# Single-tile experts: the down product in plain fp32, its weights read in place at a register's address

## The chip, the cores and the metric

One Trainium2 chip, one of its NeuronCores. The metric is the device time of one execution in microseconds. Engines are called TensorE (PE, with its weight loads as PEld), VectorE (DVE), ScalarE (ACT), GpSimd (POOL) and SyncE (SP, which issues DMAs).

## The reference

The kernel computes four stages on x (16 blocks of 128 rows, 256 wide) with a context of the same shape, each added to x after a layer norm: a masked context product, a transformer block whose feed-forward part has 8 experts (top 2), a cross-attention, and a second layer of 16 experts (top 2) with a shared one. The change lies in the first layer of experts:

```
w = vals / jnp.sum(vals, axis=-1, keepdims=True)          # vals, idx: top 2 of 8
gate = jnp.sum(jax.nn.one_hot(idx, E) * w[..., None], axis=1)
hid = silu(einsum('td,edf->tef', t, w1)) * einsum('td,edf->tef', t, w3)
y_e = einsum('tef,efd->ted', hid, w2)                     # the down product
y = einsum('ted,te->td', y_e, gate)
```

t has 2048 rows of 256, an expert is 512 wide. All is fp32.

## The kernel before

Rows are sorted by expert through DRAM, and each tile of 128 rows is computed for one expert only. The first layer (r = 0) has NT0 = 39 tiles. The first PAIRED = 18 go in pairs that share weights; the 21 after them (j = 18 to 38) are the single tiles. Which expert a tile has is known only at run time: TI[j, 0] holds its number, and an engine that needs it loads it into a register (value_load) and addresses the weights with it. WGU and WD hold the gate/up and the down weights of all experts in SBUF.

A single tile goes through these phases:
- SP: xs fetches the tile's rows.
- PE: xT transposes them (2 matmuls, lines 954 and 955); ACT: xT_e copies the result (L1332).
- ACT and DVE: wa and wv (L1307, L1855) copy the two halves of the expert's gate/up weights, scaled by g2, into one of two buffers; both wait for up(j-2) and then load the expert's number.
- PE: gate and up, eight plain fp32 matmuls each (L982).
- ACT: silu (L1338); DVE: hm multiplies it with up into H_ (two buffers, L1879).
- The split: ACT rounds the weights of down (wdh, L1316) and the hidden values (hh, L1350) to fp32r, and DVE takes the remainders (wdl, L1872, and hl, L1888). There is one buffer for the split weights.
- PE: down adds three fp32r products for each of four k (mm3, L788 to L790) in one bank.
- DVE: y copies the bank out (L1896); SP: ys stores it to DRAM.

The order of the work on each engine is fixed when the program is built. A planner (Plan.order, lines 144 to 196) keeps a clock for each engine and takes, over all engines, the phase with the least sum of its earliest start and its due time. A phase's due time is 3j plus its entry in LEAD: 100 for xT, gate and up, 300 for hm, 200 for wv, 300 for wa, -17200 for xT_e; down has none. A phase's successor on another engine is ready when it has ended and 200 more (170 after DVE) have passed, on the same engine after 60. The costs are nanoseconds written in the code; they set nothing but the order:

```
k = min(starts, key=lambda k: starts[k] + phases[k][4])
t = starts[k]
engine, ns, _, banks, _, late = phases[k]
```

PSUM has eight banks; in this stage xT, gate, up and down have two each, and a bank is used again when its reader has emptied it.

After the last single tile comes the cross-attention. Its K and V products (lines 1031 and 1041, by mm3) can begin beside the last tiles, in two banks that K_e and V_e (L1416, L1426) empty into buffers which lie on top of WD; the first of these evictions wait for wdl(38), the last reader of WD. Q needs x, so it waits for the experts' results: all y stored, then gathered by GpSimd (ga, L2148), weighted and normed (pro1, pro2: L1938, L1941, L1957), transposed (NT).

Of the kernel before, what the change touches and what calls it, by code (L numbers as in the profile page):

```python
# [12 lines left out]
ACT = mybir.ActivationFunctionType  # L13
# [3 lines left out]
D = 256  # L17
# [106 lines left out]
class Plan:  # L124
# [9 lines left out]
    def add(self, engine, ns, key, *after, banks=(), due=0, late=None):  # L134
        after = [k for k in after if all(not isinstance(i, int) or i >= 0 for i in k)]
        name = (engine, key[0], key[1] if key[0] in BY_STAGE else 0)
        due += LEAD.get(key[0] + str(key[1]) if key[0] in BY_STAGE else key[0], 0) + NUDGE.get(key, 0)
        if name in self.latest:
            after.append(self.latest[name])
        self.latest[name] = key  # L140
        assert key not in self.phases, key
        self.phases[key] = (engine, ns, after, banks, due, LATE.get(engine, 200) if late is None else late)
# [141 lines left out]
def expert_phases(p, r, start):  # L284
    F, n = F_[r], 2 * F_[r]
    nd, ny = ((1, 3), (2, 3))[r]
    for j in range(NT_[r]):
        def add(engine, ns, name, *after, banks=(), **kw):
            p.add(engine, ns, (name, r, j), *after, banks=[(ring + str(r), (q, r, j)) for ring, q in banks],
                  due=3 * j, **kw)  # L290
        begin = start if j == 0 else []
        add("SP", 1000, "xs", ("xT", r, j - 3), *([("ix", r, j - 3)] if r else []), *begin, late=28000 if r and j < 3 else 2200)
        if not r and j < PAIRED:
            j0 = j - j % 2
            add("ACT", 960, "wa", ("up", r, j - 2), *begin)
            add("DVE", 1145, "wv", ("wa", r, j))
            if j == j0:
                add("ACT", 960, "wdh", ("down", r, j - 1), *begin)
                add("DVE", 1145, "wdl", ("wdh", r, j))
            add("PE", 220, "xT", ("xs", r, j), banks=[("xT", "xTl")])  # L300
            add("ACT", 310, "xTh", ("xT", r, j), ("up", r, j0 - 3))
            add("DVE", 420, "xTl", ("xTh", r, j))
            p.add("PE", 1440, ("gate", r, j), ("xTl", r, j0), ("wv", r, j), ("xTl", r, j0 + 1), banks=[("gate0", ("silu", r, j))], due=3 * j)
            add("PE", 1440, "up", ("gate", r, j), banks=[("up", "hm")])
            add("ACT", 470, "silu", ("gate", r, j), ("hl", r, j - 2))
            add("DVE", 600, "hm", ("up", r, j), ("silu", r, j))
            add("ACT", 520, "hh", ("hm", r, j), ("down", r, j0 - 1))
            add("DVE", 600, "hl", ("hh", r, j))
            add("PE", 1440, "down", ("hl", r, j0 + 1), ("wdl", r, j0), banks=[("down", "y")])
            add("DVE", 345, "y", ("down", r, j), *([("ys", r, j - ny)] if j >= ny else []))  # L310
            add("SP", 60, "ys", ("y", r, j), late=2000)
            continue
        add("ACT", 100 + 0.84 * n, "wa", ("up", r, j - 2), *begin)
        add("DVE", 60 + 0.6 * n, "wv", ("up", r, j - 2), *begin)
        add("ACT", 100 + 0.84 * n, "wdh", ("down", r, j - nd), *begin)
        add("DVE", 70 + 1.04 * n, "wdl", ("wdh", r, j))
        add("PE", 220, "xT", ("xs", r, j), banks=[("xT", "xT_e")])
        add("ACT", 270, "xT_e", ("xT", r, j), ("up", r, j - 2))
        add("PE", 3.52 * F, "gate", ("xT_e", r, j), ("wv", r, j), ("wa", r, j), banks=[("gate", "silu")])
        add("PE", 3.52 * F, "up", ("gate", r, j), banks=[("up", "hm")])  # L320
        add("ACT", 62 + 0.79 * F, "silu", ("gate", r, j), ("hl", r, j - 2))
        add("DVE", 70 + 1.04 * F, "hm", ("up", r, j), ("silu", r, j))
        add("ACT", 90 + 0.84 * F, "hh", ("hm", r, j), ("down", r, j - 1))
        add("DVE", 70 + 1.04 * F, "hl", ("hh", r, j))
        add("PE", 2.82 * F, "down", ("hl", r, j), ("wdl", r, j), banks=[("down", "y")])
        add("DVE", 330, "y", ("down", r, j), *([("ys", r, j - ny)] if j >= ny else []))
        if r:
            add("DVE", 100, "ix", ("xs", r, j), *([("te",)] if j == 0 else []))
            add("POOL", 1100, "ys", ("y", r, j), ("ix", r, j), late=2000)
        else:  # L330
            add("SP", 60, "ys", ("y", r, j), late=2000)
# [7 lines left out]
def cross_phases(p):  # L339
    p.add("SP", 100, ("load_kv",), ("down", 0, PAIRED - 1), due=0, late=12000)  # L340
    p.add("SP", 100, ("load_q",), ("down", 0, NT0 - 1), late=8000)
    p.add("ACT", 100, ("tanh",), ("load_kv",), ("hh", 0, NT0 - 1))
    p.add("DVE", 330, ("btg",), ("tanh",))
    over = [("wa", 0, NT0 - 1), ("wv", 0, NT0 - 1)]
    for j in range(-1, NB // 2):
        due = 3 * (j + 1)

        def add(engine, ns, key, *after, banks=(), **kw):
            p.add(engine, ns, key, *after, banks=banks, due=due, **kw)
# [16 lines left out]
        for u in range(2):  # L366
            n = 2 * j + u
            if j in EARLY_KV:
                add("SP", 60, ("kl", n), ("S", 2 * (n - 3) + 1), late=2500)
                for h in (4 * j + 2 * u, 4 * j + 2 * u + 1):  # L370
                    add("SP", 60, ("vl", h), ("PV", h - 7), late=2500)
                continue
            for half in range(2):
                add("PE", 1440, ("K", j, u, half), ("kwl", u), ("cl", j), ("S", 2 * (n - 3) + 1), banks=[("proj", ("K_e", j, u, half))])
                add("ACT", 466, ("K_e", j, u, half), ("K", j, u, half), ("S", 2 * (n - 3) + 1), *([("wdl", 0, NT0 - 1)] if n < 3 else []))
            for i in range(2):
                add("PE", 1380, ("V", j, u, i), ("vwl", u), ("K", j, 0, 0), ("PV", 4 * j + 2 * u + i - 7), banks=[("proj", ("V_e", j, u, i))])
                add("ACT", 466, ("V_e", j, u, i), ("V", j, u, i), ("PV", 4 * j + 2 * u + i - 7), *([("wdl", 0, NT0 - 1)] if 4 * j + 2 * u + i < 7 else []))
        for b in (2 * j, 2 * j + 1):
            add("POOL", 2550, ("ga", 0, b), ("ys", 0, NT0 - 1), ("places",), ("pro1", b - 2),  # L380
                late=4000 if b < 2 else 2800)
# [109 lines left out]
def program(nc, a, out):  # L491
    with ExitStack() as ctx:
# [135 lines left out]
        def done(*key):  # L628
            return S[SIGNAL[key[0]]], ORD[key]
# [162 lines left out]
        def tensor(pe):  # L792
# [193 lines left out]
            def down(r, j):  # L986
                F, n, D_ = F_[r], 2 * F_[r], WDN_[r]
                vacant(pe, "down", r, j)
                hT, wd, at, step = HT_[r][0], D_[j % len(D_)], 0, 128
                if paired(r, j):  # L990
                    pe.wait_ge(*done("hl", r, j - j % 2 + 1))
                    pe.wait_ge(*done("wdl", r, j - j % 2))
                    hT, at, step = HTP, 128 * (j % 2), 256
                else:
                    pe.wait_ge(*done("hl", r, j))
                    pe.wait_ge(*done("wdl", r, j))
                for k in range(F // 128):
                    i = mm3(pe, ps("down", r, j)[:, 0:D],
                            [hT[:, (i * F // 128 + k) * step + at:(i * F // 128 + k) * step + at + 128] for i in range(2)],
                            [wd[:, i * n + k * D:i * n + k * D + D] for i in range(2)], k == 0, k == F // 128 - 1)  # L1000
                i.then_inc(*fills("down", r, j))
# [195 lines left out]
        def scalar(act):  # L1197
# [136 lines left out]
            def silu(r, j):  # L1334
                act.wait_ge(*full("gate", r, j))
                if j >= 2:
                    act.wait_ge(*done("hl", r, j - 2))
                act.activation(H_[r][j % 2], ps("gate", r, j)[:, 0:F_[r]], ACT.Silu).then_inc(*frees("gate", r, j))  # L1338

            def hh(r, j):  # L1340
# [68 lines left out]
            def K_e(jj, u, half):  # L1409
                n = 2 * jj + u  # L1410
                act.wait_ge(*full("K", jj, u, half))
                if n >= 3:
                    act.wait_ge(*full("S", 2 * (n - 3) + 1, i=1))
                else:
                    act.wait_ge(*done("wdl", 0, NT0 - 1))
                act.copy(kT_[n % 3][:, half * 512:half * 512 + 512],  # L1416
                         ps("K", jj, u, half)[:, :]).then_inc(*frees("K", jj, u, half))

            def V_e(jj, u, b2):
                n = 4 * jj + 2 * u + b2  # L1420
                act.wait_ge(*full("V", jj, u, b2))
                if n >= 7:
                    act.wait_ge(*full("PV", n - 7))
                else:
                    act.wait_ge(*done("wdl", 0, NT0 - 1))
                act.copy(xv_[n % 7], ps("V", jj, u, b2)[:, :]).then_inc(*frees("V", jj, u, b2))  # L1426

            def Q_e(jj, u, half):
# [954 lines left out]
```

## Time and profile before

| what | value |
|---|---|
| median of 3 runs | 919.88 us (916.21 to 920.40) |
| span of the profiled execution | 928.5 us; the page gives no other time of it |
| TensorE busy | 863.3 us, 93% of the span |
| VectorE, ScalarE, GpSimd busy | 710.4, 607.8, 278.9 us |
| single tiles of the first experts | 299 to about 411 us of the span |

Times in the rows are microseconds from the start of the span. Busy is the sum of an engine's instructions; a matmul's record lasts longer than its spacing, because matmuls are pipelined, so the distance between starts is what one costs. One plain fp32 matmul of the program leaves two records. "Idle before <- releaser" is the time that the engine stood still ahead of an instruction and what ended it; "issue" is a wait for which the profile shows no releaser.

### The profile page before, as it was taken

How to read it: one execution, taken by the hardware profiler on the slowest of the kernel's cores; microseconds unless marked ns; L12 is line 12 of the kernel's file. 1: busy time of each engine (PE TensorE's matmuls, PEld its weight loads, DVE VectorE, ACT ScalarE, POOL GpSimd, SP SyncE). 2: the span in 40 equal slices, each digit the busy share in tenths (PEclk: the TensorE clock that was granted, in tenths of full speed). 3: DMA queues.
4: the chain of work that ended last, by engine and by line, in shares of the span. 5: the costliest groups of instructions: out<-in, count | busy, mean ns of one | idle time of the engine just before them, and what ended most of it. 6: DMA issues, size and time to landing. Idle time of an engine off the chain costs nothing.

```text
span 928.5 us, 23435 instructions
## 1 busy us (share of the span) xinstructions
PE 863.3 (93%) x7788; PEld 771.5 (83%) x7788; DVE 710.4 (77%) x1976; ACT 607.8 (65%) x1719; POOL 278.9 (30%) x359
## 2 busy tenths in 40 slices
PE   5899988758999999998899999999999999999997
PEld 3677666437999999997799988899888989999996
DVE  5888888656898666675788888977678548888867
ACT  4488899735766666665667676677766326777740
POOL 4755578640000000004432333511113102333320
PEclk9999999958999999999999999999999999999999
DMA  9145701611111411103100122121024952333335
GB/s 327 64 177 217 291 25 36 264 55 52 52 62 55 149 53 46 53 24 127 39 24 24 45 84 58 62 66 35 25 102 161 412 123 87 99 96 102 99 117 196
DMA packets 43031, 97.11 MB, mean 105 GB/s; under 512 B 6080, under 2 KB 28480, under 8 KB 41504
## 3 DMA queue, kind: packets, MB, share of 16 engines
q1 hardware_dynamic: 36048, 76.81, 23.8%
q0 software_dynamic: 6864, 18.80, 5.8%
q8 instruction: 64, 1.05, 0.5%
q14 instruction: 55, 0.45, 0.2%
HBM read 62.22 MB, written 33.37 MB: 103 GB/s over the span
## 4 chain that ended last, share of the span: by engine, by line
PE 64%; DVE 7%; issue 3%; ACT 2%; another core or an unknown queue 1%; POOL 1%; DMA 1%; ACTq 0%; DVEq 0%; POOLq 0%
PE ps L982 17%; PE ps L788 11%; PE ps L790 10%; PE ps L789 10%; PE ps L1099 3%; PE ps L1075 3%; PE ps L1085 3%; PE ps L1157 2%; DVE BIGR L1903 1%; PE ps L954 1%; PE ps L955 1%; ACT BIG L1443 1%; DVE BIG L1980 1%; DVE X L1938 1%
## 5 line engine op out<-in xcount | busy, mean ns | idle before, releaser
L788 PE MATMUL ps<-BIGR 128*128 128x256 f32 (+1 forms) x970 | 299.0, 308 | 10.5 <-DVE BIGR L1903 3.9
L790 PE MATMUL ps<-BIGR 128*128 128x256 f32 (+1 forms) x922 | 263.4, 286 | 0.0
L789 PE MATMUL ps<-BIGR 128*128 128x256 f32 (+1 forms) x746 | 219.2, 294 | 0.0
L788 PEld LDWEIGHTS ps<-BIGR 128*128 128x128 f32 x970 | 186.0, 192 | 20.1 <-issue 16.1
L982 PE MATMUL ps<-BIG 128*128 128x128 f32 x1424 | 180.5, 275 | 0.0
L790 PEld LDWEIGHTS ps<-BIGR 128*128 128x128 f32 x922 | 176.5, 191 | 0.7
L982 PEld LDWEIGHTS ps<-BIG 128*128 128x128 f32 x1424 | 169.9, 192 | 0.1
L789 PEld LDWEIGHTS ps<-BIGR 128*128 128x128 f32 x746 | 143.9, 193 | 1.9
L2148 POOL DMA_INDIRECT BIG<-ys_dram,YI x32 | 34.4, 1076 | 221.6 <-DMA ys_dram<-BIG 213.6
L1443 ACT ACTIVATE BIG<-ps,BIG 128x128 f32<-128x128 f32 x256 | 91.4, 384 | 13.9 <-DVE BIG L1983 13.7
L2134 POOL DMA_INDIRECT xs_dram<-TT,PI x64 | 67.0, 1046 | 73.7 <-ACT PI L1284 59.3
L2156 POOL DMA_INDIRECT yt_dram<-BIG,IX x47 | 45.8, 974 | 124.0 <-DVE BIG L1896 121.2
L1872 DVE TENSOR_TENSOR BIGR<-BIG,BIGR 128x512 fp32r<-128x512 f32 (+1 forms) x77 | 69.3, 900 | 14.1 <-ACT BIGR L1316 9.1
L1251 ACT ACTIVATE BIG<-ps,BIG 128x128 f32<-128x128 f32 x256 | 71.6, 407 | 6.4 <-DVE BIG L1578 6.3
L2070 POOL TENSOR_TENSOR st<-st,CS 128x1 f32<-128x1 f32 (+1 forms) x48 | 30.8, 647 | 120.9 <-DVE st L1533 120.8
L789 PE MATMUL ps<-CTR,BIGR 128*128 128x256 f32 x224 | 63.2, 282 | 0.0
L1316 ACT CAST BIGR<-BIG 128x512 fp32r (+1 forms) x77 | 60.0, 781 | 1.5 <-PE ps L790 0.8
L1443 ACT ACTIVATION_READ_ACCUMULATOR BIG<-ps,BIG 128x1 f32 x256 | 56.9, 222 | 0.0
L1903 DVE TENSOR_TENSOR BIGR<-BIG,BIGR 128x1024 fp32r<-128x1024 f32 (+3 forms) x61 | 52.0, 870 | 6.1 <-ACT BIGR L1304 3.5
L1451 ACT COPY BIG<-ps 128x512 f32<-128x512 f32 x64 | 38.6, 603 | 22.4 <-PE ps L1085 13.8
L1307 ACT COPY BIG<-BIG 128x512 f32 x47 | 29.1, 619 | 34.3 <-PE ps L982 32.9
L1578 DVE TENSOR_REDUCE BIG<-ps 128x4 f32<-128x512 f32 x64 | 41.7, 678 | 11.2 <-PE ps L891 7.6
(264 smaller groups left out, 1870.5 us busy)
## 6 DMA issues: line engine op xcount, KB each, us to landing
BIG<-in_wgu SPq DMA_DIRECT2D x2, 6144.0 KB, 19.1
BIG<-in_wd SPq DMA_DIRECT2D x2, 4096.0 KB, 22.6
BIG<-xs_dram SPq DMA_DIRECT2D x47, 129.5 KB, 2.1
xs_dram<-CT SPq DMA_DIRECT2D x8, 640.0 KB
BIG<-xs_dram SPq DMA_DIRECT2D x39, 128.0 KB, 2.0
ys_dram<-BIG SPq DMA_DIRECT2D x39, 128.0 KB, 1.7
BIG<-in_wkv SPq DMA_DIRECT2D x2, 2048.0 KB, 9.0
kv_dram<-BIG SPq DMA_DIRECT2D x16, 256.0 KB, 2.1
```

Source lines behind the costliest of these rows:

```text
L788: pe.matmul(o, l[0], r[0], start=start, stop=False)
L789: pe.matmul(o, l[0], r[1], start=False, stop=False)
L790: return pe.matmul(o, l[1], r[0], start=False, stop=stop)
L982: i = pe.matmul(o[:, c * 128:(c + 1) * 128], wt[:, at:at + 128], x[:, k * 128:(k + 1) * 128], start=k == 0, stop=k == 1)
L1251: i = act.activation(p_[g][:, at], ps("s", b, i=g)[:, at], ACT.Exp, bias=sm[:, 4 * g + n:4 * g + n + 1])
L1316: act.copy(D_[j % len(D_)][:, 0:n], WD[:, bass.ds(e * n, n)]).then_inc(S["down_hi"], 1)
L1443: i = act.activation(xp_[s % 4][:, at], ps("S", s // 2, i=s % 2)[:, at], ACT.Exp, bias=sm[:, 4 + n:5 + n], accum_out=sm[:, 8 + n:9 + n])
L1578: v.tensor_reduce(sm_[b % 2][:, 4 * g:4 * g + 4], ps("s", b, i=g)[:, :].rearrange("p (n t) -> p n t", n=4), AX, ALU.max, negate=True).then ...
L1872: v.tensor_tensor(wd[:, n:2 * n], WD[:, bass.ds(e * n, n)], wd[:, 0:n].bitcast(F32), ALU.subtract).then_inc(S["down_lo"], 1)
L1903: return v.tensor_tensor(dst, src, hi.bitcast(F32), ALU.subtract)
L2134: pool.indirect_dma_start(XS if r else XS0, bass.IndirectOffsetOnAxis(ap=PI[:, b, k:k + 1], axis=0), TT[tile_of(r, b)][:, 0:ROW if r else ...
L2156: pool.indirect_dma_start(YT, bass.IndirectOffsetOnAxis(ap=IX[:, j:j + 1], axis=0), Y_[1][j % 3], None).then_inc(sem(f"results_placed{j % ...
```

## The change

For r = 0 and a single tile, wdh, wdl, hh and hl are gone. Down waits for hm(j), loads the expert's number on TensorE, and makes four plain fp32 matmuls with H_ stationary and WD moving, read in place. What waited for hl or wdl now waits for down. For paired tiles and for r = 1 nothing is changed.

```diff
 (expert_phases: the planner's view of a single tile)
-        add("ACT", 100 + 0.84 * n, "wdh", ("down", r, j - nd), *begin)
-        add("DVE", 70 + 1.04 * n, "wdl", ("wdh", r, j))
+        if r:
+            add("ACT", 100 + 0.84 * n, "wdh", ("down", r, j - nd), *begin)
+            add("DVE", 70 + 1.04 * n, "wdl", ("wdh", r, j))
...
-        add("ACT", 62 + 0.79 * F, "silu", ("gate", r, j), ("hl", r, j - 2))
+        add("ACT", 62 + 0.79 * F, "silu", ("gate", r, j), ("hl" if r or j - 2 < PAIRED else "down", r, j - 2))
         add("DVE", 70 + 1.04 * F, "hm", ("up", r, j), ("silu", r, j))
-        add("ACT", 90 + 0.84 * F, "hh", ("hm", r, j), ("down", r, j - 1))
-        add("DVE", 70 + 1.04 * F, "hl", ("hh", r, j))
-        add("PE", 2.82 * F, "down", ("hl", r, j), ("wdl", r, j), banks=[("down", "y")])
+        if r:
+            add("ACT", 90 + 0.84 * F, "hh", ("hm", r, j), ("down", r, j - 1))
+            add("DVE", 70 + 1.04 * F, "hl", ("hh", r, j))
+            add("PE", 2.82 * F, "down", ("hl", r, j), ("wdl", r, j), banks=[("down", "y")])
+        else:
+            add("PE", 3.42 * F, "down", ("hm", r, j), banks=[("down", "y")])
 (cross_phases: tanh after silu(38) in place of hh(38); the first K_e and V_e after down(38) in place of wdl(38))
 (down)
-                else:
+                elif r:
                     pe.wait_ge(*done("hl", r, j))
                     pe.wait_ge(*done("wdl", r, j))
+                if not r and not paired(r, j):
+                    pe.wait_ge(*emptied("up", r, j))
+                    if j == PAIRED:
+                        pe.wait_ge(sem("tiles_listed"), 1)
+                        pe.wait_ge(sem("wd_loaded"), 16)
+                    e = pe.value_load(TI[j:j + 1, 0:1], min_val=0, max_val=E0 - 1)
+                    for k in range(4):
+                        i = pe.matmul(ps("down", r, j)[:, 0:D], H_[r][j % 2][:, k * 128:k * 128 + 128],
+                                      WD[:, bass.ds(e * n + k * D, D)], start=k == 0, stop=k == 3)
+                    i.then_inc(*fills("down", r, j))
+                    return
 (silu)
-                    act.wait_ge(*done("hl", r, j - 2))
+                    act.wait_ge(*(done("hl", r, j - 2) if r or paired(r, j - 2) else full("down", r, j - 2)))
 (K_e and V_e, the first ones)
-                    act.wait_ge(*done("wdl", 0, NT0 - 1))
+                    act.wait_ge(*full("down", 0, NT0 - 1))
```

emptied("up", r, j) is signalled by hm(j), which reads up's bank last.

## Rows read from the trace of the kernel before

**Rows 1.** The page: the span, and each engine's busy time.
```profile
span 928.5 us, 23435 instructions
PE 863.3 (93%) x7788; PEld 771.5 (83%) x7788; DVE 710.4 (77%) x1976; ACT 607.8 (65%) x1719; POOL 278.9 (30%) x359
```

**Rows 2.** Busy time by stretch: stretch, length, engines, granted clock, DMA share, GB/s.
```profile
0.00:50.00 50.00, 36.17 (x259) 27.98 (x259) 35.04 (x117) 24.61 (x63) 30.57 (x50) 1.00 0.52 187
183.00:207.00 24.00, 13.62 (x69) 7.78 (x70) 11.78 (x55) 8.78 (x29) 12.25 (x14) 0.51 0.16 56
299.00:410.00 111.00, 110.31 (x950) 108.54 (x950) 75.05 (x106) 72.72 (x104) 0.00 (x0) 1.00 0.21 67
434.00:438.00 4.00, 2.00 (x9) 1.14 (x7) 3.22 (x11) 2.23 (x5) 2.46 (x3) 1.00 0.00 0
```

**Rows 3.** Groups by line, 299 to 410: count, busy, mean ns, idle before.
```profile
L982 PE MATMUL ps<-BIG 128*128 128x128 f32 x656 | 79.9, 275 | 0.0
L1872 DVE TENSOR_TENSOR BIGR<-BIG,BIGR 128x1024 fp32r<-128x1024 f32 x20 | 24.5, 1225 | 7.3 <-ACT BIGR L1316 7.3
L1316 ACT CAST BIGR<-BIG 128x1024 fp32r x21 | 21.9, 1042 | 0.0
L788 PEld LDWEIGHTS ps<-BIGR 128*128 128x128 f32 x84 | 15.9, 189 | 2.5 <-issue 2.5
```

**Rows 4.** Instructions in order of time, 372 to 377: start, length, engine, line.
```profile
372.59 1.95 PE L982 MATMUL ps<-BIG 128*128 128x128 f32 x16
...
373.20 1.23 DVE L1872 TENSOR_TENSOR BIGR<-BIG,BIGR 128x1024 fp32r<-128x1024 f32 x1 [0.38 <-ACT BIGR L1316]
...
374.54 0.19 PEld L788 LDWEIGHTS ps<-BIGR 128*128 128x128 f32 x1 [0.20 <-issue]
374.57 0.36 PE L788 MATMUL ps<-BIGR 128*128 128x256 f32 x1
...
375.21 1.15 ACT L1307 ACTIVATE BIG<-BIG,small 128x1024 f32 x1 [1.40 <-PE ps L982]
...
375.31 0.75 DVE L1855 TENSOR_SCALAR BIG<-BIG,small 128x1024 f32 x1 [0.89 <-PE ps L982]
...
375.98 0.68 DVE L1879 TENSOR_TENSOR BIG<-ps,BIG 128x512 f32<-128x512 f32 x1
376.08 1.95 PE L982 MATMUL ps<-BIG 128*128 128x128 f32 x16
```

**Rows 5.** In order of time: gate(19), then gate(38) with up(38).
```profile
306.13 1.95 PE L982 MATMUL ps<-BIG 128*128 128x128 f32 x16
...
408.24 3.73 PE L982 MATMUL ps<-BIG 128*128 128x128 f32 x32
```

**Rows 6.** Chain of waits, line 1157: start, length; x8 counts records.
```profile
763.24 1.73 PE ps L1157 x8
```

**Rows 7.** Lines 1292 and 1307, ScalarE's register load: lengths in ns, least, median, most.
```profile
L1292 ACTq TENSOR_LOAD <-TI x77: 275/284/712, 208.6 to 886.7; - x77
L1292 ACTq TENSOR_LOAD <-TI x1: 276/276/276, 374.6 to 374.6; - x1
L1292 ACTq FUSED_REGOPS  x1: 152/152/152, 374.9 to 374.9; - x1
L1307 ACTq FUSED_REGOPS  x1: 55/55/55, 375.1 to 375.1; - x1
```

**Rows 8.** A wait of TensorE's queue at line 1027, and down(37)'s first matmul.
```profile
L1027 PEldq EVENT_SEMAPHORE  x1: 1409/1409/1409, 411.7 to 411.7; - x1
...
411.73 0.36 PE L788 MATMUL ps<-BIGR 128*128 128x256 f32 x1
```

**Rows 9.** Chain of waits from the last down on: start, length, what.
```profile
418.63 0.44 DVE BIG L1896
...
438.36 0.36 PE ps L788
```

More of the change, by code:

```diff
@@ L341, in cross_phases @@
     p.add("SP", 100, ("load_q",), ("down", 0, NT0 - 1), late=8000)
-    p.add("ACT", 100, ("tanh",), ("load_kv",), ("hh", 0, NT0 - 1))
+    p.add("ACT", 100, ("tanh",), ("load_kv",), ("silu", 0, NT0 - 1))
     p.add("DVE", 330, ("btg",), ("tanh",))
@@ L374, in cross_phases @@
                 add("PE", 1440, ("K", j, u, half), ("kwl", u), ("cl", j), ("S", 2 * (n - 3) + 1), banks=[("proj", ("K_e", j, u, half))])
-                add("ACT", 466, ("K_e", j, u, half), ("K", j, u, half), ("S", 2 * (n - 3) + 1), *([("wdl", 0, NT0 - 1)] if n < 3 else []))
+                add("ACT", 466, ("K_e", j, u, half), ("K", j, u, half), ("S", 2 * (n - 3) + 1), *([("down", 0, NT0 - 1)] if n < 3 else []))
             for i in range(2):
                 add("PE", 1380, ("V", j, u, i), ("vwl", u), ("K", j, 0, 0), ("PV", 4 * j + 2 * u + i - 7), banks=[("proj", ("V_e", j, u, i))])
-                add("ACT", 466, ("V_e", j, u, i), ("V", j, u, i), ("PV", 4 * j + 2 * u + i - 7), *([("wdl", 0, NT0 - 1)] if 4 * j + 2 * u + i < 7 else []))
+                add("ACT", 466, ("V_e", j, u, i), ("V", j, u, i), ("PV", 4 * j + 2 * u + i - 7), *([("down", 0, NT0 - 1)] if 4 * j + 2 * u + i < 7 else []))
         for b in (2 * j, 2 * j + 1):
@@ L1424, in V_e @@
                 else:
-                    act.wait_ge(*done("wdl", 0, NT0 - 1))
+                    act.wait_ge(*full("down", 0, NT0 - 1))
                 act.copy(xv_[n % 7], ps("V", jj, u, b2)[:, :]).then_inc(*frees("V", jj, u, b2))
```

## The prediction

> **What bounds the kernel now.** Read the page first: the span and the busy shares [rows 1]. TensorE is busy 93% of the span, so a change pays or costs where it moves TensorE's work or its waits. Then the table by stretch [rows 2]: the tiles that the change touches run from 299 to about 411 us, and there TensorE is busy 110.31 of 111.00 us at a granted clock of 1.00 (2.4 GHz), while VectorE has 75 and ScalarE 73 us. What the change takes from VectorE and ScalarE was therefore waiting time of engines that had room; what it adds to TensorE counts in full.
>
> The lines of that stretch [rows 3] give the durations. Gate and up are line 982: a plain fp32 matmul leaves two records, so each of gate and up has 16. The split down product is lines 788 to 790, 12 records a tile. One stall of TensorE shows: 2.5 us in 11 waits ahead of L788.
>
> The order in time [rows 4] says why. TensorE repeats gate (16 records), transpose (2), up (16), then down of the tile before (12): up(31) at 372.59, down(30) at 374.57, gate(32) at 376.08. VectorE's split copy L1872 ran from 373.20 to 374.43, and down's weight load began at 374.54 after 0.20 of idling: down was waiting for the split copy, in every second tile. From gate(19) at 306.13 to gate(38) at 408.24 [rows 5] it is 102.11/19 = 5.37 us a tile.
>
> **Removed.** 21 single tiles (18 to 38) lose L1316 (1.04 us) and L1350 on ScalarE, L1872 (1.23) and L1888 on VectorE [rows 3]. Neither engine bounds the stage, so this pays only through the waits: the 2.5 us ahead of L788, and the end of the stage, below.
>
> **The product itself.** Split: from 374.57 to 376.08, 1.51 us. Plain fp32 with 256 columns stands elsewhere in this trace: line 1157 does the same shape, four matmuls in 8 records in 1.73 us [rows 6]. So +0.22 us a tile, 4.6 us over 21 tiles, if nothing else moved.
>
> **The register.** TensorE now loads the expert's number in every tile, behind its wait for hm(j). No register load of TensorE is in the trace; ScalarE and VectorE do the same load ahead of L1307 and L1855; on ScalarE it is [rows 7] 0.276 us TENSOR_LOAD, 0.152 register arithmetic, a check, 0.055 for the address. Up(31) ends at 372.59 + 1.95 = 374.54; L1307 starts at 375.21 and L1855 at 375.31 [rows 4], 0.67 and 0.77 us after their release. I take 0.67 for TensorE. Bounds: 0, if the load runs ahead of the wait; 0.67 + 0.44 = 1.11, if it costs as much as ScalarE's longest load (0.712 in place of 0.276 [rows 7]). The three later addresses, 0.06 each, lie beside matmuls of 0.43 (two records); exposed they would be 0.2 a tile, 4 us in all. The Trainium skill (DMA: Bandwidth & Descriptors, section Latency and other measured facts) gives about 600 ns as the floor of such a load; the row with 0.276 is below it, and by it the forecast would be an estimated 6 us later.
>
> Whether that 0.67 counts depends on how early the wait ends. TensorE's queue takes instructions long before they run: the wait of line 1027 began at 411.7, when the first of the 12 products ahead of it was only starting at 411.73, and lasted 1.41 us beside them [rows 8]. So a load whose wait is over costs nothing; one behind a late wait is exposed whole.
>
> **The order decides.** The planner takes at each step the phase with the least (earliest start + due), due = 3j + its LEAD. Before, down(j) became ready after hm, hh and hl and so ran behind up(j+1). Now it hangs on hm(j) alone. In the planner's own units, from the end of up(j): VectorE is free for wv(j+2) after the 200 of lateness (LEAD 200, hm has 300, so wv goes first), 674, then hm 602, then 170 of lateness: down(j) is ready at 1646. Gate(j+1) ends at 3.52 x 512 = 1802. At 1802 down(j) stands at 3j, the transpose of the next tile at 3(j+2) + 100, up(j+1) at 60 + 3(j+1) + 100. Down(j) is taken, ahead of up(j+1). By the same rule the transposes fall behind up, two in every second tile, since up(j+1) (103) then beats one of them (106).
>
> On the chip hm(j) is later than the planner thinks, since it counts no register load on VectorE. Up(31) ends at 374.54, wv runs at 375.31, hm from 375.98 to 376.66 [rows 4]: 2.12 us after up's end. Gate(j+1)'s records start 0.16 before that end (0.275 of duration, 0.11 apart) and last 16 x 0.1115 = 1.78, so TensorE is free at +1.62. Down then waits for hm (+2.12), has its load exposed (+0.67) and starts at about +2.83. It takes 1.73, up 1.78, and the last record ends 0.16 later: +6.50 is the next up's end. Where the two transposes come first, gate starts 0.73 late and ends at +2.5, still under this wait. The 0.20 before L788 goes and a wait of 1.2 us takes its place. A tile costs 6.50 in place of 5.37, +1.13.
>
> Sum: 19 tiles from the end of up(19) to that of up(38) x 1.13 = 21.5. At the entry down(18) (1.73) now goes ahead of up(19), its load hidden beside the paired products: +1.7. At the end, before, 418.63 - 411.97 = 6.66 us lie between up(38)'s end (408.24 + 3.73) and y(38), line 1896 [rows 5, 9]; in it down(37), two K groups, a wait and down(38). Down(37) is now counted in a period, and down(38) starts at the +2.83 that two K groups take anyway: y at +4.7, so -1.9. From y the chain goes on as before: store, gather, and so to Q at 438.36 [rows 9]. Total +21.3 us.
>
> The new waits of K_e and V_e (for the last down, no longer wdl) hold K_e by about a down and its hand-over, some 2 us; behind it on ScalarE are the other evictions, and TensorE's V groups wait for the two banks. That is covered: TensorE is busy only 2.00 of the 4 us to 438 [rows 2], waiting for what the gather brings. If that cover were gone it would cost 2 us. The granted clock should stay at 2.4 GHz: it was 1.00 from 0 to 50 us too, where TensorE idled far more (36.17 of 50 us busy); the row with 0.51 is one in which it was busy 13.62 of 24 [rows 2].
>
> The span of the profiled execution, 928.5 us, is the only time that the page gives; it is 8.6 above the median of the runs, 919.88. Against it the sum is 949.8; on the median, adding the same, 941.2. I forecast 941.
>
> **Rivals.** (a) Down(j) stays behind up(j+1): then hm (+2.12) is over before up(j+1) is done and the load is hidden. The sum is 21 x 0.22 = 4.6 less 2.5 of stall less 1.9 at the end, +0.2: 920, not slower; it is faster than 915 only if the new order of the later phases gains 5 us besides. It decides if hm(j) in the plan is ready later than 1802. For it: down is there now. Against: 1646. The Trainium skill (Advanced Engine Details and Errata, sections Sequencer Loop and Engine Queue Depths) has TensorE queue 64 instructions, and others queued while the sequencer works; by that rule the load costs nothing and this rival's 920 follows; the row of line 1027 agrees that the queue runs far ahead, but a queue helps only when the wait is over.
> (b) Down(j) goes ahead of up(j+1), but hm(j) runs before wv(j+2) on VectorE: hm ends at +0.72, the load is over before gate. A tile is then 1.78 + 1.73 + 1.78 and half of the transposes' 0.89, 5.74: 19 x 0.37 + 1.7 - 1.9 = +6.8: 927. Against it: LEAD 200 against 300.
> (c) My order, but the load free: down starts at +2.2 (or +2.5 behind transposes), 0.48 less a tile: +12, 932. Dearer, 1.11 and the later addresses exposed: +21.3 + 8.4 + 4 = +34, 954.
>
> **Chances.** My case, with the load from free to dear, 0.76; (a) 0.15, of it 0.04 faster; (b) 0.09. About 0.5%, 4.6 us, is what a measurement can tell. Range 925 to 954: it leaves out (a) and some 5 in 100 on the far side, where the new order of all later phases costs something too. The order of the cross-attention stage shifts with this, by a few us either way; that is in it. Faster 0.04, the same 0.11, slower 0.85.
>
> **What would show it.** In the changed profile: 8 records of 1.73 us for down; gate, down, up in that order, not gate, up, down; a wait of about 1.2 us on TensorE ahead of down in each of 19 tiles, released by line 1879 with the load behind it; 6.5 us a tile; transposes in pairs; VectorE and ScalarE under half busy in the stage. No wait ahead of down, or down behind the next up, proves me wrong, and so does a period under 5.7.

## The result and the profile after

The changed kernel takes 945.31 us (944.5 to 945.61, 4 runs) where the kernel before takes 918.66 (916.21 to 920.4) on the same chip: ratio 1.0303, 95% interval 1.0278 to 1.0329. It is slower, as forecast, and by 26.7 us where 21.3 were forecast; 945 lies inside the range, 941 was the number.

The one profiled execution of before that the prediction had was nearly 13 us longer than a second one, whose span is 915.8 us. In the second one gate(18) starts at 292.32 us, up(38) ends at 405.24 and y(38) starts at 411.90. Differences below are taken against that one, whose stage is as long as in [rows 5]. Gate(18) and y(38) in it, then in the changed kernel, where the way between them is 148.83 us in place of 119.58:

```profile
292.32 1.95 PE L982 MATMUL ps<-BIG 128*128 128x128 f32 x16
...
411.90 0.42 DVE L1896 COPY BIG<-ps 128x256 f32<-128x256 f32 x1 [1.55 <-PE ps L790]
...
291.42 1.95 PE L986 MATMUL ps<-BIG 128*128 128x128 f32 x16
...
440.25 0.43 DVE L1911 COPY BIG<-ps 128x256 f32<-128x256 f32 x1 [2.68 <-PE ps L1008]
```

The page of the changed kernel, span and busy line, answers to [rows 1]. VectorE lost 38.5 us of work and ScalarE 31.4, and the span grew:

```profile
span 943.2 us, 23268 instructions
PE 867.4 (92%) x7704; PEld 770.2 (82%) x7704; DVE 671.9 (71%) x1934; ACT 576.4 (61%) x1677; POOL 278.2 (29%) x359
```

Busy time of its single-tile stage, columns as in [rows 2]. TensorE now idles 17.2 of 137 us where it idled 0.7 of 111; the granted clock is still 1.00, and VectorE and ScalarE are busy under a third:

```profile
299.00:436.00 137.00, 119.78 (x859) 110.19 (x860) 39.38 (x64) 43.47 (x64) 0.00 (x0) 1.00 0.16 52
```

Its instructions in order of time, down(29) to down(30), answer to [rows 4]. L986 is gate and up, L1008 down, L1870 wv, L1894 hm, L958 the first half of a transpose:

```profile
374.96 0.68 DVE L1894 TENSOR_TENSOR BIG<-ps,BIG 128x512 f32<-128x512 f32 x1
...
376.56 1.99 PE L1008 MATMUL ps<-BIG 128*128 x8 [1.27 <-DVE BIG L1894]
...
378.39 1.95 PE L986 MATMUL ps<-BIG 128*128 128x128 f32 x16
...
380.18 0.27 PE L958 MATMUL ps<-CS,BIG 128*128 128x128 f32 x1
...
381.06 2.02 PE L986 MATMUL ps<-BIG 128*128 128x128 f32 x16 [0.29 <-issue]
...
381.11 0.76 DVE L1870 TENSOR_SCALAR BIG<-BIG,small 128x1024 f32 x1 [2.09 <-PE ps L986]
...
381.78 0.68 DVE L1894 TENSOR_TENSOR BIG<-ps,BIG 128x512 f32<-128x512 f32 x1
...
383.39 1.99 PE L1008 MATMUL ps<-BIG 128*128 x8 [0.30 <-issue]
...
385.21 1.05 PE L986 MATMUL ps<-BIG 128*128 128x128 f32 x8
```

Down(29) at 376.56 runs ahead of up(30) at 378.39, and TensorE stood idle for 1.27 us before it, released by hm. The second product, 383.39, shows only 0.30 of idling, because the transposes of two tiles pushed gate back; it starts no earlier for that. From 376.56 to 383.39 it is 6.83 us a tile, against 5.37 before. The gap between hm's end (374.96 + 0.68 = 375.64) and the product is 0.92 us. In it lies the register's load on TensorE's queue, here the two of this stretch (columns: times in ns, least, median, most):

```profile
L1006 PEldq TENSOR_LOAD <-TI x2: 313/314/314, 375.8 to 382.6; - x2
L1006 PEldq FUSED_REGOPS  x2: 151/151/151, 376.2 to 383.0; - x2
```

And the waits from 299 to 440 us (engine, line, releaser: us in total, times, longest). The weight loads of down wait 20.4 us in 21 tiles, and TensorE waits for hm in ten of them; VectorE, with less work, waits 55.8 us for down ahead of y (L1911):

```profile
DVE BIG L1911 <- PE ps L1008: 55.8, 20, 3.1
...
PEld ps L1008 <- issue: 20.4, 21, 1.8
PE ps L1008 <- DVE BIG L1894: 13.4, 10, 1.6
```

### The profile page after: what moved, and what is told of

It reads as the page before. It is cut to its first block, busy times and chain, and to the rows that moved or that the text cites. A ratio compares the mean times of both kernels' runs of the same rounds, so it can differ in the third digit from the quotient of the medians.

```text
span 943.2 us, 23268 instructions
## 1 busy us (share of the span) xinstructions
PE 867.4 (92%) x7704; PEld 770.2 (82%) x7704; DVE 671.9 (71%) x1934; ACT 576.4 (61%) x1677; POOL 278.2 (29%) x359
## 4 chain that ended last, share of the span: by engine, by line
PE 65%; DVE 8%; issue 4%; ACT 1%; DMA 1%; DVEq 1%; POOL 0%; ACTq 0%; POOLq 0%
PE ps L986 15%; PE ps L792 10%; PE ps L793 10%; PE ps L794 10%; PE ps L1008 4%; PE ps L1090 3%; PE ps L1114 3%; PE ps L1100 3%; PE ps L1172 2%; DVE BIGR L1918 1%; PE ps L958 1%; PE ps L959 1%; DVE BIG L1894 1%; PE ps L948 1%; DVE BIG L1995 1%
## 5 line engine op out<-in xcount | busy, mean ns | idle before, releaser
L792 PE MATMUL ps<-BIGR 128*128 128x256 f32 (+1 forms) x886 | 273.4, 309 | 8.6 <-DVE BIGR L1918 3.9
L794 PE MATMUL ps<-BIGR 128*128 128x256 f32 x838 | 239.2, 285 | 0.0
L793 PE MATMUL ps<-BIGR 128*128 128x256 f32 (+1 forms) x662 | 195.2, 295 | 0.0
L792 PEld LDWEIGHTS ps<-BIGR 128*128 128x128 f32 x886 | 169.6, 191 | 16.5 <-issue 11.3
L986 PE MATMUL ps<-BIG 128*128 128x128 f32 x1424 | 179.9, 275 | 2.6 <-issue 2.6
L986 PEld LDWEIGHTS ps<-BIG 128*128 128x128 f32 x1424 | 170.6, 192 | 5.6 <-issue 4.5
L794 PEld LDWEIGHTS ps<-BIGR 128*128 128x128 f32 x838 | 160.2, 191 | 0.7
L793 PEld LDWEIGHTS ps<-BIGR 128*128 128x128 f32 x662 | 127.6, 193 | 2.0
L1911 DVE COPY BIG<-ps 128x256 f32<-128x256 f32 x86 | 36.2, 424 | 62.6 <-PE ps L1008 58.5
L1347 ACT COPY BIG<-ps 128x256 f32<-128x256 f32 x68 | 24.0, 367 | 58.2 <-PE ps L959 57.2
L1008 PE MATMUL ps<-BIG 128*128 x168 | 41.8, 391 | 16.5 <-DVE BIG L1894 13.4
```

The lines of the kernel that those rows point to most:

```text
L792: pe.matmul(o, l[0], r[0], start=start, stop=False)
L793: pe.matmul(o, l[0], r[1], start=False, stop=False)
L794: return pe.matmul(o, l[1], r[0], start=False, stop=stop)
L986: i = pe.matmul(o[:, c * 128:(c + 1) * 128], wt[:, at:at + 128], x[:, k * 128:(k + 1) * 128], start=k == 0, stop=k == 1)
L1008: i = pe.matmul(ps("down", r, j)[:, 0:D], H_[r][j % 2][:, k * 128:k * 128 + 128], WD[:, bass.ds(e * n + k * D, D)], start=k == 0, stop=k == 3)
L1911: v.tensor_copy(Y[j % len(Y)], ps("down", r_, j)[:, 0:D]).then_inc(*frees("down", r_, j))
```

## The experiments

Ratios are to the kernel before, run on the same chip. The runs used several chips, so ratios are the safer comparison between them. Profiles of one execution differ, too, in what lies ahead of the stage, which the edits do not touch: in the changed kernel and all the runs below gate(18) starts somewhere from 291.42 to 294.09 us. So differences of 1 or 2 us between two runs are not explained here.

| run | us | ratio, 95% interval |
| --- | --- | --- |
| changed kernel | 945.31 | 1.0303 [1.0278, 1.0329] |
| e1 down(j) behind up(j+1) | 920.42 | 1.0022 [1.0006, 1.0039] |
| e5 e1, constant expert | 922.42 | 1.0052 [1.0036, 1.0068] |
| e3 register loaded at gate(j) | 935.91 | 1.0193 [1.0174, 1.0212] |
| e2 constant expert | 934.67 | 1.0179 [1.0164, 1.0195] |
| e4 hm ahead of wv | 928.9 | 1.0123 [1.0105, 1.0142] |
| e6 e3 and e4 together | 925.43 | 1.0082 [1.0061, 1.0104] |
| e12 register loaded twice | 974.47 | 1.061 [1.0584, 1.0637] |
| e8 before, copies of weights first | 915.95 | 0.9981 [0.9968, 0.9994] |
| e9 e8, tile 38 alone plain | 916.02 | 0.9976 [0.9965, 0.9987] |
| e10 e9, y ahead of kwl(1), vwl(1) | 912.7 | 0.995 [0.9933, 0.9968] |
| e11 e8, hm(38) first | 917.32 | 0.9996 [0.9982, 1.001] |

**The baseline again (e0).** The kernel before, without an edit, profiled once more: 917.56 us, span 915.8.

> The kernel before, unchanged, for a second profile: the first one's span (928.5) stood about 11 us over what its other runs imply, and its clock was at 1.2 GHz from 183 to 207 us. All theories: about 918 us, span about 917; gate(18) near 291 us as in the changed kernel, not 299; from gate(19) to the last y about 112.5 us.

The 12.7 us by which the first profile was longer lie outside the stage: from gate(18) to y(38) it is 119.58 us in both. Gate(18) is 6.7 us later there, at 299.05, and 6.0 more come behind y(38). Ahead of the stage the stretch from 183 to 207 us has a granted clock of 0.51 in [rows 2] and of 0.79 here; how much of the 6.7 us that makes is not shown.

**Order alone (e1).** The plan's down waits for one phase more; code, product and register load stay:

```
- add("PE", 3.42 * F, "down", ("hm", r, j), banks=...)
+ add("PE", 3.42 * F, "down", ("hm", r, j), *([("up", r, j + 1)] if j + 1 < NT0 else []), banks=...)
```

> The changed kernel, but the planner makes down(j) wait for up(j+1) too, so that TensorE runs gate, transpose, up, down as before; fp32 product and register load stay. Theory (the order exposes hm and the load): the load hides behind up, a tile costs 5.55 in place of 6.83 us, 19 tiles, so about 921 us (917 to 925). Rival 1 (the load costs its 0.9 us wherever it stands on TensorE): a tile 6.4, about 937. Rival 2 (fp32 or the later phases cost it): 943 or more.

920.42: the order, with the register load that it exposes, is the whole loss but 2 us, and the forecast's rival (a) had the number (920), but by +0.2 us on a median of 919.88; beside the kernel before in this run, 918.15, it is +2.3. Its trace in order of time, one tile:

```profile
352.75 1.89 PE L1008 MATMUL ps<-BIG 128*128 x8
...
354.47 1.95 PE L986 MATMUL ps<-BIG 128*128 128x128 f32 x16
...
358.26 1.89 PE L1008 MATMUL ps<-BIG 128*128 x8
```

No idle time stands before down; the product takes 1.72 to 1.73 us (352.75 to 354.47), and a tile 5.51 to 5.52.

**The load moved ahead of gate(j) (e3).**

```
+ loaded[j] = pe.value_load(TI[j:j + 1, 0:1], ...)   # in gate(j), ahead of its waits
- e = pe.value_load(TI[j:j + 1, 0:1], ...)           # in down(j), behind the wait for hm
+ e = loaded.pop(j)
```

> The changed kernel in its own order, but the expert's number is loaded on TensorE ahead of gate(j), a product earlier, and kept in a register. Theory: the wait for hm stays (down at +2.2 after up's end), the 0.9 us load behind it goes, where two transposes stand ahead gate itself ends at +2.5; 0.7 less a tile over 19 tiles, about 932 us (929 to 935). Rival 1 (a load costs wherever it stands): 944 to 946. Rival 2 (the wait for hm alone is the cost, the load is hidden by the queue already): 944 to 946.

935.91, 9.4 us below the changed kernel, and 0.9 above the range expected. Its order of time, hm (L1900) and the product (L1014):

```profile
370.40 0.68 DVE L1900 TENSOR_TENSOR BIG<-ps,BIG 128x512 f32<-128x512 f32 x1
...
371.35 1.99 PE L1014 MATMUL ps<-BIG 128*128 x8 [0.61 <-DVE BIG L1900]
```

The product comes 0.27 after hm's end (371.08), not 0.92: the load is worth 0.65 us behind the wait. A tile is 6.21. From gate(18) to y(38) the gain is 12.5 us (136.36 for 148.83), which is 19 times 0.65; in the time only 9.4 are left, because in this profile gate(18) comes 2.3 us later and the rest is 1.0 us longer than in the changed kernel's, both outside what the edit touches.

**No load at all (e2, e5).** The address is a constant, in the changed kernel's order and in e1's. This leaves out the choice of the expert, so these two kernels do not compute the program's result; they serve for their times alone:

```
- WD[:, bass.ds(e * n + k * D, D)]
+ WD[:, k * D:k * D + D]
```

> The changed kernel in its own order (down(j) right behind gate(j+1)), with the choice of the expert left out: the down product always reads expert 0 at a constant address, so no register is loaded. Theory (what the load costs is that it stands behind the wait for hm on an empty queue; elsewhere it is free): the same as with the load moved ahead of gate(j), 935.9 us, so 934 to 937; down's first matmul 0.27 us after hm's end, tile 6.25 us. Rival (a load costs its length wherever it stands): 19 x 0.65 = 12 us below that, 924. Either way it stays slower than the kernel before by over 0.5%: what is left is the wait for hm itself.

> The changed kernel with down(j) planned behind up(j+1), as in the run that timed 920.42 us, and with the choice of the expert left out: the down product always reads expert 0 at a constant address, so TensorE loads no register. Theory (the register load costs time only where TensorE's queue is empty in front of it; behind up(j+1) the queue is full): the load of 0.65 us was wholly hidden there, so this runs as that kernel did, 920 us (918 to 921.5), tile 5.5 us. Rival (every register load holds TensorE up for its own length, and the 5.52 us tile contains it): 19 x 0.65 = 12 us less, 908, tile 4.9 us.

E2 took 934.67, as the first theory said: taking the load out is not told apart from moving it (their intervals overlap). The forecast's rival (c), the changed order with a free load, had priced it at 932. Down starts 0.15 after hm's end, where 0.27 was expected. E5 did not gain on e1: 922.42, 0.9 us above the range expected. From gate(18) to y(38) the two are alike (122.46 and 122.63 us); e5's profile is later by 1.7 us already at gate(18), which the edit does not touch and which stays unexplained. So behind up(j+1) the load costs nothing that these two profiles show.

**hm ahead of wv on VectorE (e4), and both repairs (e6).** After planning, PE's order kept:

```
+ at = first.index(("hm", 0, j))
+ if first[at - 1] == ("wv", 0, j + 2):
+     first[at - 1], first[at] = first[at], first[at - 1]
```

> The changed kernel with TensorE's order kept; on VectorE hm(j) runs ahead of wv(j+2) for the single tiles, so hm ends 0.7 in place of 2.1 us after up(j). Theory: wait and load end about when gate(j+1) does; a tile costs 5.75 to 5.85 us in place of 6.83, about 925 us (921 to 930). Rival 1 (the load costs its 0.9 us wherever it stands): 6.5 a tile, about 938. Rival 2 (VectorE's order is no part of it): 943 or more.

> The changed kernel with both repairs: hm(j) ahead of wv(j+2) on VectorE (928.9 us alone) and the register loaded ahead of gate(j) (935.9 alone). Theory (the two overlap: with hm(j) early, the load's end at up(j)'s end + 1.65 already lies within gate(j+1), which ends at + 1.8): 1 to 2 us less than with hm first alone, 927 (925 to 929), so the two do not add up. Rival (they are separate costs of 16.4 and 9.4 us): 945.3 - 25.8 = 919.5, the time of before.

E4: 928.9; the forecast's rival (b) had priced this order at 927. In its trace hm (L1899) is over 1.86 us before the product (L1013) behind transposes, and 0.92 before it, with no idling of TensorE, in the other tiles:

```profile
369.63 0.69 DVE L1899 TENSOR_TENSOR BIG<-ps,BIG 128x512 f32<-128x512 f32 x1 [1.36 <-PE ps L991]
...
372.18 1.89 PE L1013 MATMUL ps<-BIG 128*128 x8
...
375.89 0.69 DVE L1899 TENSOR_TENSOR BIG<-ps,BIG 128x512 f32<-128x512 f32 x1 [1.36 <-PE ps L991]
...
377.50 1.99 PE L1013 MATMUL ps<-BIG 128*128 x8
```

E6: 925.43, so the two gains (16.4 and 9.4) do not add up: 19.9 together. What is left over e1, 5 us, fits a third cost of the order, the transposes in pairs. It is read from the trace; no run takes the pairs alone away. In e6's trace nothing waits ahead of down (L1019), but up (L997) waits for ScalarE's copy of the transposes:

```profile
366.06 1.89 PE L1019 MATMUL ps<-BIG 128*128 x8
...
369.90 0.27 PE L964 MATMUL ps<-CS,BIG 128*128 128x128 f32 x1
370.42 2.05 PE L997 MATMUL ps<-BIG 128*128 128x128 f32 x16 [0.24 <-ACT BIG L1358]
372.31 1.89 PE L1019 MATMUL ps<-BIG 128*128 x8
...
377.61 1.89 PE L1019 MATMUL ps<-BIG 128*128 x8
```

The last transpose starts at 369.90 and up at 370.42, 0.52 apart where 0.11 is the distance in a full queue; a pair of tiles takes 11.55 us (366.06 to 377.61) against 2 x 5.52 = 11.04.

**The load twice (e12).**

```
  e = pe.value_load(TI[j:j + 1, 0:1], ...)
+ e = pe.value_load(TI[j:j + 1, 0:1], ...)
```

> The changed kernel with the register's load made twice in a row in front of each down product. Theory (behind the wait for hm nothing covers TensorE's control instructions, so each costs its own time; in the changed kernel's trace a load took 0.31 + 0.15 + 0.06 us): 19 to 21 x 0.5 to 0.65 = 10 to 14 us more, 957 (954 to 960), down's first matmul 1.45 us after hm's end instead of 0.92. Rival (the loads overlap, or what costs is the wait's own hand-over): 945 to 948.

974.47, 29 us more: the load's own price was right, the total was not. Down starts 1.58 to 1.61 us after hm's end, 0.66 later than with one load, and where the clock holds a tile is 7.5 us (384.70 to 399.71 for two), +0.68, so 13 us. From gate(18) to y(38) it is 174.49 us, 25.7 more than in the changed kernel; the other half of that goes with a lower clock, and some 4 us of the 29 lie outside the stage. Windows of its stage, and three products (L1009) with a gate (L986):

```profile
324.00:339.00 15.00, 11.79 (x86) 1.00 0.12 37
339.00:354.00 15.00, 11.44 (x68) 0.89 0.08 27
...
369.00:384.00 15.00, 12.52 (x81) 0.89 0.11 35
384.00:399.00 15.00, 11.79 (x84) 1.00 0.12 36
```

```profile
375.56 2.74 PE L1009 MATMUL ps<-BIG 128*128 x8 [1.93 <-issue]
...
378.09 2.90 PE L986 MATMUL ps<-BIG 128*128 128x128 f32 x16
...
384.70 1.99 PE L1009 MATMUL ps<-BIG 128*128 x8 [0.96 <-issue]
...
392.23 1.99 PE L1009 MATMUL ps<-BIG 128*128 x8 [1.96 <-issue]
```

After 1.93 us of idling the product takes 2.53 us (375.56 to 378.09) where 1.83 is usual, and the gate behind it 2.74 (378.09 to 380.83) where 1.78 is: part of this ran at 1.2 GHz, in a stretch whose granted clock is 0.89. An idle time as long, 1.96 us ahead of 392.23, left the clock at 1.00. From 339 us on the granted clock is below 1.00 in eight of nine stretches of 15 us, 0.89 in six of them; in the changed kernel it is 1.00 in all of the stage. One more load a tile was enough to bring a second loss, which the changed kernel does not have.

**What of the change is worth keeping (e8 to e11).** All four start from the kernel before. E8 only swaps neighbours in two orders, so that the copies of the weights come ahead of those of the hidden values:

```
+ for engine, early, late in (("ACT", "wdh", "hh"), ("DVE", "wdl", "hl")):
+     if order[at + 1] == (early, 0, j):            # at: index of (late, 0, j)
+         order[at], order[at + 1] = order[at + 1], order[at]
```

> The kernel before with one thing changed: on the single tiles ScalarE makes wdh(j) ahead of hh(j), and VectorE wdl(j) ahead of hl(j), where they stood the other way round. Theory: the copies of the expert's weights need no product of the tile, so they end earlier and down(j) never finds them late; the one stall of 2.0 to 2.5 us ahead of a down product in the stage of the single tiles goes, and hl(j), which now comes last, is ready before up(j+1) has ended: 916 us (914 to 918), 2 us below before. Rival: hl(j) becomes late because the copies stand in front of it, by up to the 0.4 us of a copy on 19 tiles: 918 + 7 = 925.

915.95, as expected: from gate(18) to gate(38) it is 106.48 us, against 109.19 in the second profile of before; the stall ahead of L788 of [rows 3] is gone, and a tile is 5.23 us.

E9 adds the change for tile 38 alone (register loaded at gate(38), K products behind down(38)); e10 moves ("kwl", 1) and ("vwl", 1) behind ("y", 0, 38) in VectorE's order; e11 leaves the split everywhere and moves ("hm", 0, 38) ahead of ("kwl", 0).

> The kernel before with the copies of the weights ahead of hh and hl as in the run beside it, and with the change made for tile 38 alone: its down product in plain fp32 with the weights read in place, its register loaded ahead of gate(38), no split copies; the first K product stands behind it. Theory (the chain hm, hh, hl, down, y of the last tile has nothing to stand behind, so there, and there alone, leaving hh and hl out shortens the way to the end): y(38) comes up(38)'s end + 3.7 us where it was + 6.7, so some 3 us earlier, 2 to 3 us below the run with the order alone: 913 us (911 to 916). Rival (what follows y(38) waits for something else, or the K products lose as much as y(38) gains): the same as the run with the order alone, 916.

> The run with the last tile alone in plain fp32 (916.02 us), with one thing moved: VectorE makes y(37) and y(38) ahead of the low halves kwl(1) and vwl(1), not behind them. In that run's profile down(38) started at 405.53 us and was over by about 407.3, but VectorE read it at 409.87 only, because four such halves (4.62 us) stood in front. Theory (what the plain product freed at the last tile was given to another engine's queue): y(38) comes 2.2 us earlier, down(38)'s start + 2.1 instead of + 4.3, and with it the rest: 914 us (912 to 915.5). Rival (the stage behind it waits for its K products, not for y(38)): 916.

> The kernel before with the copies of the weights ahead of hh and hl (915.95 us) and hm(38) moved ahead of kwl(0) on VectorE, with the split copies kept on all tiles. In the profile of that run up(38) ended at 403.0 us but hm(38) started at 405.58, behind 2.4 us of low halves. Theory: hm(38) starts 2.4 us earlier, but its weights' copies (ending at 407.4) then come last, so the last down product starts 0.7 us earlier (408.10 to 407.4) and the time is 915.3 (913.5 to 916.5), not to be told from 916. Rival (the whole 2.4 us reach the end): 913.5.

E9 gained nothing over e8 (916.02): the rival's number, but not its reason, since y(38) itself was held. VectorE's order of time in e9 shows what held it: y(37) and y(38) (L1921, two in one row) stand behind four low halves (L1928), although down(38) started at 405.53:

```profile
404.91 4.62 DVE L1928 TENSOR_TENSOR BIGR<-BIG,BIGR 128x1024 fp32r<-128x1024 f32 x4
409.45 0.75 DVE L1921 COPY BIG<-ps 128x256 f32<-128x256 f32 x2
```

In e10 (L1932 and L1925 there) only two stand in front, and both y are over by 407.78:

```profile
404.76 2.35 DVE L1932 TENSOR_TENSOR BIGR<-BIG,BIGR 128x1024 fp32r<-128x1024 f32 x2
407.03 0.75 DVE L1925 COPY BIG<-ps 128x256 f32<-128x256 f32 x2
407.69 2.35 DVE L1932 TENSOR_TENSOR BIGR<-BIG,BIGR 128x1024 fp32r<-128x1024 f32 x2
```

912.7 us: it beats both kernels, by 0.5% [0.9933, 0.9968] against before. From gate(38) to y(38) it is 6.98 us, 9.25 in e9, 10.39 in e8. The place of y alone does not do it: in e8 y(38) (L1903) already stands ahead of the second pair of low halves (L1910) and waits for TensorE's split product:

```profile
409.81 0.42 DVE L1903 COPY BIG<-ps 128x256 f32<-128x256 f32 x1 [1.54 <-PE ps L797]
410.15 2.35 DVE L1910 TENSOR_TENSOR BIGR<-BIG,BIGR 128x1024 fp32r<-128x1024 f32 x2
```

E11 missed: 917.32, where 915.3 was expected; by its interval it is not told apart from e8. Its hm(38) did move to 403.11, but the copies did not end earlier:

```profile
403.11 0.69 DVE L1889 TENSOR_TENSOR BIG<-ps,BIG 128x512 f32<-128x512 f32 x1 [0.45 <-PE ps L992]
...
404.63 1.05 ACT L1326 CAST BIGR<-BIG 128x1024 fp32r x1 [0.83 <-PE ps L800]
...
406.32 1.22 DVE L1882 TENSOR_TENSOR BIGR<-BIG,BIGR 128x1024 fp32r<-128x1024 f32 x1
407.45 0.69 DVE L1898 TENSOR_TENSOR BIGR<-BIG,BIGR 128x512 fp32r<-128x512 f32 x1
```

The last of them, hl (L1898), ends at 408.14, in e8 at 408.00: it stands behind wdl (L1882). The copies of the weights wait for the one buffer that down(37) frees: wdh (L1326) runs on ScalarE from 404.63 to 405.68, and wdl then waits until 406.32 for VectorE, which still has low halves and y(37) to do. So on tile 38 hm's place alone does not pay; leaving the copies out, with y ahead of the low halves, does.

## Why the prediction was right, step by step

**The order.** Gate(j+1), down(j), up(j+1) and paired transposes came as worked out from the planner's units, and e1 shows that this alone decides: 920.42 without it, 945.31 with it. The wait of 1.2 us that was to stand ahead of down in each of 19 tiles stands there in ten; in the others the pair of transposes fills most of it.

**hm's time.** Forecast 2.12 us after up(j)'s end; in the changed kernel 2.13 (up(29) ends at 373.51, hm at 375.64).

**The exposed load: mis-sized.** I took 0.67 from ScalarE's start after its release; down was to start at +2.83 (2.12 and 0.67 make 2.79; the other 0.04 has no source in the forecast) and starts at +3.05. The hand-over from hm to the product is 0.92 in the changed kernel: 0.27 that a product waits even with its register ready (e3), and 0.65 for the load. I had let the one figure stand for both. The instruction itself, 0.313 us, was near ScalarE's 0.276 [rows 7]. The Trainium skill (DMA: Bandwidth & Descriptors, section Latency and other measured facts) gives some 600 ns as the least for such a load: the record of the instruction is half of that, but what a load adds to the path, 0.65 here and 0.66 a second time in e12, lies just above it.

**The product: mis-sized a little.** Forecast 1.73 from [rows 6]; where the queue is full it is that (e1, e6), behind the wait it is 1.83 (376.56 to 378.39).

**The sum.** A tile was to cost 6.50 and costs 6.83; 0.22 of the 0.33 is the load's hand-over, 0.10 the product. One of the 19 tiles, the last, has no wait, since two K groups stand ahead of gate(38); without them it is 5.60. From up(19)'s end to up(38)'s it is 131.86 us, of which 2.90 are two K groups that now run ahead of gate(38), against 101.88: +27.1 (forecast +21.5). Entry: from up(18)'s end to up(19)'s 9.35 us against 7.08, +2.3 (forecast +1.7). Exit: y(38) comes 3.67 us after up(38)'s end against 6.66 before, where +4.7 was forecast; but the two K groups ran there before, so that their new place and the exit together give -0.1, not -1.9. From gate(18) to y(38): 148.83 - 119.58 = +29.3, where the forecast's terms make 21.3. What lies before and behind the stage came out 0.9 and 1.0 us shorter, which the forecast did not foresee; by that much the total came nearer to 941 by luck.

**What a tile is made of.** The runs build it up from e1: 5.52 with the order repaired; +0.25 for paired transposes (e6, 5.77); +0.44 for hm behind wv (e3, 6.21); +0.62 for the load behind that wait (6.83). From gate(18) to y(38) these are 122.62, 128.17, 136.36 and 148.83 us, so the steps of a tile times 19 (4.8, 8.4, 11.8) come close to each step; in times, 920.4, 925.4, 935.9, 945.3. The forecast saw the transposes as lying under the wait; they do, and by e6's trace cost their own 5 us once the wait is gone.

**The rival from the queue.** Rival (a) had the load free because TensorE's queue runs ahead; behind up(j+1) it is free (e5 beside e1), behind an open wait it is paid whole (e3, e12). That condition was in the forecast and decided rightly.

**The clock** held at 1.00, as forecast, but that was less safe than the stretch from 0 to 50 us made me think. There TensorE was busy 36.17 of 50 us at 1.00; e12, with 0.66 us more of idling a tile, is busy 11.79 of 15 us from 324 to 339 and then loses it.

## What to carry to other kernels

Taking work off engines that had room paid here only through the order in which the bounding engine then met its operands; when a planner sets that order, work the new order out in its own units before anything else. The register load was free where matmuls were still queued in front of it and cost its whole 0.65 us behind an open wait, so place it ahead of the phase before. The shorter chain was worth having where nothing stood to run beside it, at the last tile, and only once the freed time was not taken by other work in front of its reader.

## What was not expected of the hardware

- A register load behind a wait adds up without overlap: 0.92 us from hm to the product with one, 1.58 to 1.61 with two, 0.27 with the register ready, 0.15 with a constant address.
- The eight records of the down product take 1.73 us in a full queue and 1.80 to 1.83 when the first starts on an idle engine (e2, and the changed kernel).
- The granted clock, 1.00 in all of the changed kernel's stage, was 0.89 in six of e12's nine stretches of 15 us from 339 us on. In one of them the engine had idled 1.93 us ahead of a down product, and the product behind that idling took 2.53 us in place of 1.83; after 1.96 us of idling in a stretch at 1.00 it took 1.82.
